# Extra matrix products with no reader in a four-layer kernel, ahead of two fences and inside a threshold search

## The reference, cut to what matters

```
xn = layernorm(x)
x  = x + attention_like(xn) * silu(ffn_like(xn))
```

```
logits = flat_x @ gate_w.T                      # 2048 tokens, 16 experts
scores = softmax(logits).T                      # 16 x 2048
topk_weight, topk_idx = top_k(scores, 256)      # per expert, capacity 256
... each expert's products on its 256 tokens, scatter-added ...
shared = (gelu(xn @ Sg.T) * (xn @ Su.T)) @ Sd.T
```

## Time and profile before

| what | value |
|---|---|
| median of 3 runs | 1961.46 us (1961.2 to 1962.14) |
| span of the profiled execution, first to last instruction | 1957.4 us |
| what lies around the span, median less span | 4.06 us |
| PE busy | 1744.6 us, 89% |
| DVE busy | 1421.3 us, 73% |
| ACT busy | 1155.9 us, 59% |
| POOL busy | 1040.4 us, 53% |
| mean granted clock of TensorE | 0.951 |
| Layer 2, from its first DMA to its last sum | 1312.1 to 1564.3 us of the span |

### The profile page before, as it was taken

One profiled execution on the slowest core, in us unless ns is written; L12 is line 12 of the kernel. 1 busy time (PEld: TensorE's weight loads), 2 busy tenths in 40 slices (PEclk: granted clock), 3 DMA queues, 4 the chain that ended last, 5 costly groups with the idle time before them and its releaser, 6 DMA issues. The chain is left out here.

```text
span 1957.4 us, 34440 instructions
## 1 busy us (share of the span) xinstructions
PE 1744.6 (89%) x13171; PEld 1433.1 (73%) x13199; DVE 1421.3 (73%) x2911; ACT 1155.9 (59%) x2340; POOL 1040.4 (53%) x998
## 2 busy tenths in 40 slices
PE   6999999999999999899799788874798568999997
PEld 4888888888888888787567577763577445666676
DVE  6888888788888788534578677857767488777772
ACT  4677767676767777555367555552433344666665
POOL 4888999999999999920312134335257530110111
PEclk9999999999999999999889899986799878999999
DMA  3000000001000000000000000002045300000000
GB/s 90 14 1 15 1 15 1 15 1 36 1 1 1 1 1 1 28 1 1 20 11 22 1 2 2 2 23 69 23 109 133 78 12 1 2 2 2 2 2 23
DMA packets 52100, 37.44 MB, mean 19 GB/s; under 512 B 7560, under 2 KB 45864, under 8 KB 51936
## 3 DMA queue, kind: packets, MB, share of 16 engines
q1 hardware_dynamic: 45248, 30.53, 5.3%
q0 software_dynamic: 5632, 4.20, 1.5%
q10 hardware_dynamic: 1056, 0.52, 0.1%
HBM read 29.99 MB, written 5.24 MB: 18 GB/s over the span
## 5 line engine op out<-in xcount | busy, mean ns | idle before, releaser
L753 POOL TENSOR_TENSOR dtl<-dts,dth 128x512 fp32r<-128x512 f32 x256 | 356.5, 1392 | 20.5
L683 DVE TENSOR_REDUCE nm<-PS 128x1 f32<-128x1024 f32 x256 | 311.6, 1217 | 30.5 <-PE PS L203 29.6
L1930 ACT ACTIVATE ET_a<-PS 128x256 f32<-128x256 f32 (+2 forms) x512 | 223.0, 493 | 129.2 <-PE PS L1845 78.6
L751 POOL CAST dth<-dts 128x512 fp32r<-128x512 f32 x256 | 232.6, 909 | 48.6 <-ACT dts L610 47.5
L201 PE MATMUL PS<-xh,yh 128*128 128x512 f32 x512 | 225.5, 440 | 8.1 <-ACT G L603 4.0
L144 PE MATMUL PS<-C,XN 128*128 128x128 f32 x1120 | 176.3, 283 | 38.1 <-DVE XN L196 34.6
L203 PE MATMUL PS<-xh,yl 128*128 128x512 f32 x512 | 204.7, 400 | 0.0
L202 PE MATMUL PS<-xl,yh 128*128 128x512 f32 x512 | 204.4, 399 | 0.0
L1744 POOL TENSOR_SCALAR_AFFINE_SELECT ET_a<-ET_a 128x1024 f32<-128x1024 f32 x32 | 35.0, 1092 | 310.3 <-ACT ET_a L1930 310.3
L603 ACT ACTIVATE XNT<-PS,nm 128x1024 f32<-128x1024 f32 x128 | 142.8, 1115 | 68.5 <-DVE nm L683 67.3
L610 ACT ACTIVATE dts<-PS 128x512 f32<-128x512 f32 x256 | 152.7, 598 | 45.9 <-POOL dtl L753 43.1
(11 more groups left out here) (425 smaller groups left out, 4709.4 us busy)
## 6 DMA issues: line engine op xcount, KB each, us to landing
e_wg<-in_WgT SPq DMA_DIRECT2D x16, 256.0 KB, 2.8
e_wu<-in_WuT SPq DMA_DIRECT2D x16, 256.0 KB, 3.1
e_wd<-in_WdT SPq DMA_DIRECT2D x16, 256.0 KB, 4.0
X<-in_L_attn_X SPq DMA_DIRECT2D x2, 512.0 KB, 4.5
wqn<-in_L_attn_Wq SPq DMA_DIRECT2D x8, 128.0 KB, 2.1
wkn<-in_L_attn_Wk SPq DMA_DIRECT2D x8, 128.0 KB, 2.6
wvn<-in_L_attn_Wv SPq DMA_DIRECT2D x8, 128.0 KB, 2.4
won<-in_WoT SPq DMA_DIRECT2D x8, 128.0 KB, 2.6
```

The source lines that it names most:

```text
L683: e.tensor_reduce(self.nm[:, half, i:i + 1], self.S[half], AX.X, MAX, negate=True).then_inc(*self.top.up((g, half)))
L751: e.tensor_copy(hi, src).then_inc(*ts.up((g, g4, "h")))
L753: e.tensor_tensor(lo, src, f(hi), SUB).then_inc(*ts.up((g, g4, "l")))
L1930: e.activation(dst, src, ACT.Exp, scale=self.SC, bias=0.0).then_inc(*self.ex.up(it))
```

## The change

A helper issues n products of the constant identity (128x128, f32) with the constant `band` (128x512, f32) into a bank that nobody reads then. Five of them stand on PE's queue ahead of the fence of Layer 2 (bank 6), fourteen ahead of the fence of Layer 3 (bank 3), and one behind the count's product in each of the rounds 2 to 13 of the search (bank 2). They wait for no semaphore and raise none. Nothing is removed or moved, and no other engine's queue is touched.

```
@@ -142,6 +142,11 @@
     def tr(self, e, o, i):
         n = i.shape[0]
         return e.transpose(o, i, self.ident[0:n, 0:n])
+
+    def keep_awake(self, e, b, n):
+
+        for _ in range(n):
+            e.matmul(self.bank(b), self.ident, self.cst("band"), start=True, stop=True)
 
     def fence(self, q):
 
@@ -1182,6 +1187,10 @@
 
     def pe(self, e, q):
         k = self.k
+        if self.tag == 2:
+            k.keep_awake(e, 6, 5)
+        elif self.tag == 3:
+            k.keep_awake(e, 3, 14)
         k.fence(q)
         for c in range(4):
             for j in range(4):
@@ -2524,6 +2533,8 @@
             elif what == "count":
                 q.wait_ge(self.find, ("count", n, 2))
                 e.matmul(B1[:, 0:3], same, self.cn3[:, :], start=True, stop=True).then_inc(*self.find_pe.up(n))
+                if 2 <= n < 14:
+                    k.keep_awake(e, 2, 1)
             elif what == "sup":
                 ms = slice(128 * n, 128 * n + 128)
                 q.wait_ge(self.in_s, 2)
```

## The result

The changed kernel takes 1965.28 us (median of 20 runs, 1961.17 to 1968.43) where the kernel before takes 1961.62 us (20 runs, 1959.83 to 1963.83): a ratio of 1.0017, 95% interval 1.0010 to 1.0023. That is 3.7 us slower in the medians. The effect is small, but the interval leaves out no change, so its sign is certain.

A forecast was written before the change was run, and what follows sets the result against it. DVE was taken as busiest in the search, PE counting only where DVE or ACT waits for a product. Terms -0.2+1.3+1.4+0.7+0.3-0.5+0 = +3.0 us gave 1964.5 us, range 1959.8 to 1967.8.

The forecast's parts named there:

- The places: Whole kernel: clock below full only in Layer 2's first half and between Layers 2 and 3, so only there can it pay.
- Price of a product: One added 128x512 f32 product on PE: 0.85 us at full clock, 1.7 us at half.
- Layer 2's fence: Five products ahead of Layer 2: hidden in PE's idle time, -0.2 us, bounds -1.4 and +2.7.
- Round 2: Search: product at half clock ahead of `sup` delays a Gelu without slack, +1.3 us, bounds 0.4 and 1.7.
- Round 3 and rounds 5 to 10: Search: delays covered by DVE's own work or its 4.23 us of idle time, 0 us.
- Round 4: Search: product ahead of the Gelu delays Sin, POOL's chain and round 8's statistics, +1.4 us, middle of 0.85 and 1.95.
- Rounds 11 and 12: Late search: round 12's count held up behind round 11's products, +0.7 us; round 12's product and `sup`, +0.3 us.
- `take`: After the search: more work ahead may keep the clock up for `take` and network products, -0.5 us, bounds -1.2 and 0.
- Layer 3's fence: Fourteen products ahead of Layer 3 end 10.5 us early, clock low again at 1570: 0 us, bounds -3.0 and +1.4.
- The rival in which PE is off the path: Search: DVE is 73% to 96% busy, added products only fill PE's waits; 1961.5 us, chance 0.21.
- The rival of a low clock each time: Search: products ahead of awaited Gelus meet half clock each time, rounds 2, 4 and 11; +5.9 us, 1967.4 us, chance 0.28.
- The rule weighed in the prediction: Layer 2's turned tiles would let the clock go, logits starting low: +0.9 us on the sum, 1965.4 us, chance 0.02.

The follow-up runs named there:

- the run without rounds 2 and 4: Added products only in rounds 3 and 5 to 13, none in rounds 2 and 4 or at the fences, against the kernel before: ratio 1.0002.
- two-products kernel: Only the added products of rounds 2 and 4, two of the 31, against the kernel before: ratio 1.0017.
- the kernel with the fences alone: Only the 5 and 14 products ahead of the fences of Layers 2 and 3, none in the search, against the kernel before: ratio 0.9999.
- the kernel with 26 products: 26 products instead of 14 ahead of Layer 3's fence, five ahead of Layer 2's, none in the search, against the kernel before: ratio 0.9993.
- the products behind the work: The search's 12 products behind each round's `sup` or `sdown`, none at the fences, against the kernel before: ratio 0.9978, 1958.21 against 1962.91 us.
- the kernel with the last three: Only three products, behind the work of rounds 11, 12 and 13, no others, against the kernel before: ratio 1.0004.
- bridged: 26 products at Layer 3's fence plus five among its turned tiles, none at Layer 2 or in the search, against the kernel before: ratio 0.9983, 1958.55 us.

## Why the prediction was right

The range (1959.8 to 1967.8) and the side hold: forecast 1964.5, measured 1965.28; +3.0 us forecast, +3.7 measured. The forecast called this no change that can be told, leaning to slower; 20 runs of each kernel do tell it. The mechanism (an added product ahead of a Gelu that others wait for, in rounds 2 and 4 only) is the one that the experiments show. That the sum comes so close is in part luck, as the terms show. Step by step, against the profile:

- **The places.** The prediction says that the clock falls below full only in Layer 2's first half and between Layers 2 and 3. The clock line also reads 8 in three of the four slices from 930 to 1125 us, ahead of Layer 2, and in the one from 1615 to 1664 us, in Layer 3. The change adds nothing there, so no term suffers, but "can only pay there" does not follow.
- **Price of a product.** 0.85 us forecast at full clock, 0.86 measured. 1.7 at half forecast, and in round 2 the second record of the `sup` starts 1.7 us later behind the count than before; 1.5 of it reached the Gelu, since the clock rose under the last of the six records.
- **Layer 2's fence.** -0.2 us forecast; -0.1 measured from the first scaling to the first logits record, and the clock still falls to half under the logits. Right.
- **Round 2.** +1.3 forecast, +1.5 measured. Right, in size and in kind.
- **Round 3 and rounds 5 to 10.** 0 forecast; 0.0 from the Sin to round 11. Right; the cover named (4.23 us of waiting for POOL) is the one that the run without rounds 2 and 4 showed at work.
- **Round 4.** +1.4 forecast, as the middle of 0.85 and 1.95; +2.2 measured. The term was undersized by 0.8 us: PE was idle 2.93 us ahead of the round's count (forecast: about 3), and the clock did fall there, so that the slow `sup` (2.5 us for 1.4) is paid in full. The two-products kernel shows the pair of rounds 2 and 4 at 3.5 us.
- **Rounds 11 and 12.** +0.7 and +0.3 forecast as middles; -0.1 and -0.3 measured. Both were oversized. In the profiled run the clock was full from 1386 on, so the count of round 12 was not held up.
- **`take`.** -0.5 forecast, +0.1 measured. Nothing was won. The errors of rounds 11 and 12 (-1.4 us together) and of `take` (+0.6) cancel the one of round 4 (+0.8): that the sum is better than its terms is luck.
- **Layer 3's fence.** 0 forecast, 0 measured, in the trace and in the kernel with the fences alone. The reason given (10 us without work behind the last product) is half of it: with no idle time left, 26 products gave nothing either, since the slow stretch lies behind the turned tiles.

The rival in which PE is off the path falls with rounds 2 and 4. The rival of a low clock each time (+5.9 us) was nearer than it looks: its condition, round 4's `sup` at half clock and round 2's too, is met in the trace. It missed because round 11, for which it had +1.8, cost nothing, and because round 4 cost 2.2 and not 2.8. The rule weighed in the prediction (the Trainium skill, "TensorE: Matmul & The Clock Gate", Part 4: PE-mode transpose), that the full clock doesn't engage for transposes, is not borne out as it stands: in Layer 2 of the changed kernel the clock was still full in 1318.5-1320.5, after 4 us of turned tiles. Yet in Layer 3, where DVE's scalings take 5.54 us instead of 4.19 and the turned tiles stand further apart, the clock was at half by 1575 in the kernel with 26 products.

What stays open: the gain of the products behind the work differs from run to run (3.6 and 2.2 us in two profiles, the second with 0.6 from ahead of the products), what decides whether the clock falls in rounds 8 to 12 and again behind round 14 wasn't settled, and with it whether a loss in the search stays a loss.

## What to carry to other kernels

An added product is work like any other: look for the instruction behind it on its queue, and for who waits for that one. The same 12 products cost 0.2% ahead of the round's real work and gain 0.2% behind it (though what stands behind one piece of work stands ahead of the next, as in round 12 of the kernel with the last three). And a full clock is worth nothing at a stage that another engine paces; keep TensorE busy up to the stage where it is itself the bound, here the values' product 10 us behind the first turned tile, and put the extra work into waits that the profile shows.

## What the runs showed of the hardware

- The clock doesn't rise at the same place of the same work in every execution. Four of the changed kernels have no product in the search before round 11. The profile of the one with fences alone has no loss there, the other three have +1.2 us (26 products, and five ahead of Layer 2), +1.3 (bridged) and +1.4 (the last three): the clock rose at 1349.6, 1358.0 and 1355.0 us instead of 1345.6, and round 4's `sup` ran at half clock. The 20 runs of the kernel before that stand beside the result spread over 4.0 us, its 35 runs in each of two other series over 7.9 and 9.0 us. A single profile of such a stage can mislead by a third of this change's effect, a single time by more than all of it.
- One added product in round 2, two records among idle time, goes with an earlier rise: in the six kernels that have one there and none before it, ahead of the `sup` or behind it, the clock first rises 22.3 to 23.2 us after the first logits record; in the six without, 25.7 to 36.4 us after it. The product makes the `sup` behind it later all the same: in round 2 of the changed kernel PE was busy for 4.00 of 4 us at 0.50, and only the next round saw 1.00.
- The clock fell from full to half under the logits (32 records of 128x16 columns) in both kernels, 1.8 and 1.9 us after their first record, and stayed at half while PE was busy with them for 3.00 of 3.00 us. PE stood idle for 0.8 and 0.7 us just ahead of them; whether that or the narrow products let the clock go, no run here separates.
